# A layernorm, attention and gated projection layer on one NeuronCore: the next batch's x brought in with features on partitions, and the order of two groups' weight work

## The chip, the cores and the metric

One core of a Trainium2 chip. The metric is the device time of one launch in microseconds, the median of the runs. Engines: TensorE (PE), VectorE (DVE), ScalarE (ACT), GpSimd (POOL) and SyncE (SP, which issues nearly all DMAs).

## The reference

For x of shape (4, 512, 1024), all in float32:

```
xn = layernorm(x)                                        # over 1024 features
q, k, v = xn @ Wq.T, xn @ Wk.T, xn @ Wv.T                # 32 query heads, 8 key/value heads, head size 128
q, k = rmsnorm(q) * q_norm_w, rmsnorm(k) * k_norm_w
attn = softmax(q k' / sqrt(128) + slope[h] * (key - query), causal)
s = (attn v) @ Wo.T                                      # 4096 -> 1024
g = silu(xn @ W.T + bias + sum_n lora_weights[n] * 2 * (xn @ A_n.T) @ B_n.T)
return x + s * g
```

## The kernel before

**Precision and products.** Each float32 operand is split into a high part (a copy rounded to fp32r, by ACT) and a low part (operand minus high, by DVE or POOL), and every product is three matmuls, high-high, high-low and low-high (lines 507 to 510).

**Groups, steps.** The kernel runs 4 batches of 8 groups (one key/value head with its 4 query heads, one gate tile). A group n = 8 batch + g has 4 steps j = 0 to 3, one query head each. In this document a step is written batch.g.j, so 1.7.0 is batch 1, group 7, quarter 0. While group n is attended, the projection of group n + 1 (q, k, v, gate: 896 columns) is computed: a 2x2 block scheme of Strassen's kind with seven products P1 to P7 of sums of blocks of x (two token halves by two feature halves) with sums of blocks of the weights. A piece is one product for one tile of 128 tokens, 12 matmuls of 448 columns. Quarter 0 takes the pieces of P1 and P2, quarter 1 those of P6 and P7, quarter 2 those of P4, quarter 3 those of P5 and P3. Pieces end in one of two PSUM banks; ACT evacuates P1 and P2 (line 827), DVE adds the others into `raw` (line 1314).

**A step on PE** (lines 704 on): scores of head m mixed with probabilities times v of head m - 1; transposes of queries and keys; the pieces; output projection of head v = m - 2, columns 0 and 1; transposes of m's probabilities, rounds 0 to 2; output columns 2; round 3; output column 3. A turned tile goes through three banks in turn: ACT takes the high part (line 858), DVE the low part (line 1284) and frees the bank. Output columns are added by DVE (`add_out`, lines 1342 and 1344), which frees the bank for the next but one.

**Orders written out by hand.** Each engine runs a list; an instruction behind a waiting one waits too.
- ACT in a step: exps, head output, queries and keys high, normalising, `split_b(v + 1)` (output weights' high part, line 822; in quarter 0 behind P1's evacuation), evacuations or squares, rounds 0 to 2 of the probabilities, high parts of one product's weights (line 788), round 3, high parts of a second product's weights (not in quarter 2).
- POOL in a step: bias of the next head (line 1100; two buffers, so it waits only for the scores of the head before), `low_b(v + 1)` (line 1092), in quarters 1 and 3 of groups 1 to 5 of batch 0 the four sums of the weights of group n + 2 (lines 1132 to 1137), then two low parts for each of the weight products that ACT has split (line 1081), the ones that PE's next step begins with. In group 0 the sums come last.
- DVE in a step: scores with bias and maxima (line 1319), inverse row sums, head output, queries low, RMS factors (lines 1262 to 1267) and scalings (line 1274), pieces, `add_out` columns 0 and 1, rounds 0 to 2 low, column 2, round 3, column 3. In quarter 2 the factors of the next group stand between columns 0 and 1. In 0.0.0 it also makes the eight weight sums of group 1, and four inverses of the gate.
- SP: loads, stores and copies in the order of their use. The sums of a group's weights go to DRAM once all four are there, and the loads of later weights wait for that store.

**x of the next batch.** The first batch's x is prepared before the steps. For batches 1 to 3, one DMA brings 512 tokens on 128 partitions; DVE takes bn_stats in quarter 1 of group 5 (group 6 for batch 1), factors in the quarter after; ACT scales and shifts the four token tiles; PE transposes x in 14 rounds of 4 transposes (`turn_x`), four in quarter 3 of group 6, six in 7.0 and four in 7.1; ACT takes the high parts (14 of 512 columns) and DVE the low parts from PSUM; POOL makes the four sums of blocks in place between rounds (P7's in 6.3, those of P6, P5 and P3 in 7.0).

## Time and profile before

| what | value |
|---|---|
| median of 3 runs (lowest, highest) | 2655.3 us (2654.26, 2657.38) |
| the profiled execution, its own time | 2655.72 us |
| its span in the trace, mean granted clock | 2653.9 us, 0.995 |
| PE, DVE, ACT, POOL busy | 97%, 64%, 66%, 65% |
| chain that ended last | PE 90%, DVE 3%, DMA 2%, POOL 2%, ACT 1% |
| DMA | 414.78 MB |

The span is the time between the first and the last instruction of the profiled execution. A window's row gives, for a stretch, the busy time of PE, PE's weight loads, DVE, ACT and POOL with their instructions, then the granted clock, the DMA share and GB/s. Starts are us from the span's start. Where a stretch of a timeline waited, the idle time before it and what ended it stand in brackets. A step's start is that of its first score matmul.

### The profile page before, as it was taken

The page shows a single profiled execution, that of the slowest core. Times are in us where ns is not written, and L with a number is a line of the kernel's source. Part 1 is how long each engine was busy: PE and PEld are TensorE (multiplying, and loading weights), DVE is VectorE, ACT ScalarE, POOL GpSimd, SP SyncE. Part 2 cuts the span into 40 slices and gives each one's busy share as a digit, 9 for nine tenths or more (in the row PEclk, how much of TensorE's full clock was granted, in tenths as well). Part 3 has the DMA queues.
Part 4 walks back from the last instruction along what each step waited for, and adds up shares of the span by engine and source line. Part 5 has one row for each costly group of instructions (what it writes and reads, how often), then busy time and mean ns, then how long its engine had stood idle before and what let it go on. Part 6 is the DMA issues. An engine that isn't in the chain of part 4 may idle for free.

```text
span 2653.9 us, 39893 instructions
## 1 busy us (share of the span) xinstructions
PE 2583.1 (97%) x13840; PEld 2288.9 (86%) x13840; DVE 1699.8 (64%) x3533; ACT 1764.6 (66%) x4633; POOL 1718.0 (65%) x839
## 2 busy tenths in 40 slices
PE   6789999999999999999999999999999999999997
PEld 5778888888888888888888888888888888888886
DVE  7565656666766665666667666666666756656656
ACT  4565666767767666667766667666777666667764
POOL 3577887785767565655667756565666766656555
PEclk9899999999999999999999999999999999999999
DMA  7868878875354333433344433433334533333323
GB/s 283 289 219 278 265 261 272 271 258 166 118 171 154 113 106 118 140 112 118 106 137 155 128 119 111 144 106 118 109 104 137 189 106 108 115 116 112 112 78 131
DMA packets 171896, 414.78 MB, mean 156 GB/s; under 512 B 31024, under 2 KB 63920, under 8 KB 170800
## 3 DMA queue, kind: packets, MB, share of 16 engines
q1 hardware_dynamic: 170144, 410.19, 47.1%
q8 instruction: 112, 1.84, 0.3%
q10 hardware_dynamic: 1552, 2.04, 0.2%
q14 instruction: 88, 0.72, 0.1%
HBM read 339.81 MB, written 89.13 MB: 162 GB/s over the span
## 4 chain that ended last, share of the span: by engine, by line
PE 90%; DVE 3%; DMA 2%; POOL 2%; ACT 1%; SPq 1%; issue 0%; ACTq 0%; POOLq 0%; DVEq 0%
PE proj L508 21%; PE proj L510 21%; PE proj L509 21%; PE tr L608 5%; PE tr L588 3%; PE sc L508 3%; PE sc L509 3%; PE sc L510 3%; PE ot L509 3%; PE ot L510 3%; PE ot L508 3%; DMA wu<-xtok 1%; PE tr L581 1%; DMA wl<-wu 1%; POOL wl L1081 1%
## 5 line engine op out<-in xcount | busy, mean ns | idle before, releaser
L1081 POOL TENSOR_TENSOR wl<-wl,wh 128x896 fp32r<-128x896 f32 x428 | 909.1, 2156 | 552.3 <-ACT wh L788 552.2
L508 PE MATMUL proj<-wh,xh 128*128 128x448 f32 x1792 | 670.7, 374 | 7.3 <-ACT raw L827 2.2
L509 PE MATMUL proj<-wl,xh 128*128 128x448 f32 x1792 | 657.9, 367 | 0.0
L510 PE MATMUL proj<-wh,xl 128*128 128x448 f32 x1792 | 657.8, 367 | 0.0
L1092 POOL TENSOR_TENSOR wb_lo<-wb_lo,wb_hi 128x1024 fp32r<-128x1024 f32 x128 | 307.7, 2404 | 303.7 <-ACT wb_hi L822 303.7
L879 ACT ACTIVATE misc<-misc,negmax 128x128 f32<-128x128 f32 (+3 forms) x512 | 286.7, 565 | 266.3 <-DVE negmax L1319 266.1
L508 PE MATMUL proj<-o_hi,wb_hi 128*128 128x512 f32 x1024 | 425.2, 415 | 7.4 <-DVE acc L1344 3.5
L1344 DVE TENSOR_TENSOR acc<-acc,proj 128x512 f32<-128x512 f32 x476 | 324.8, 683 | 149.7 <-PE proj L510 147.8
L858 ACT ACTIVATE pT_hi<-tr 128x512 fp32r<-128x512 f32 (+3 forms) x512 | 197.5, 440 | 325.9 <-PE tr L608 325.9
L510 PE MATMUL proj<-o_hi,wb_lo 128*128 128x512 f32 x1024 | 403.6, 394 | 0.0
L509 PE MATMUL proj<-o_lo,wb_hi 128*128 128x512 f32 x1024 | 401.3, 392 | 0.0
L788 ACT ACTIVATE wh<-wl 128x896 fp32r<-128x896 f32 x428 | 387.9, 965 | 19.7 <-DMA wl<-wu 19.2
L1314 DVE TENSOR_TENSOR raw<-raw,proj 128x448 f32<-128x448 f32 x320 | 197.4, 617 | 301.9 <-PE proj L510 300.1
L508 PEld LDWEIGHTS proj<-wh,xh 128*128 128x128 f32 x1792 | 337.9, 189 | 37.1 <-ACT raw L827 4.9
L510 PEld LDWEIGHTS proj<-wh,xl 128*128 128x128 f32 x1792 | 337.4, 188 | 30.0
L509 PEld LDWEIGHTS proj<-wl,xh 128*128 128x128 f32 x1792 | 338.1, 189 | 27.8
L1319 DVE CUSTOM_DVE_ANT_0 misc<-sc,misc 128x128 f32<-128x128 f32 (+3 forms) x512 | 240.9, 487 | 175.9 <-PE sc L510 174.7
L1284 DVE TENSOR_TENSOR pT_lo<-tr,pT_hi 128x512 fp32r<-128x512 f32 (+3 forms) x512 | 226.6, 484 | 74.7 <-ACT pT_hi L858 74.4
L834 ACT ACTIVATE junk<-raw 128x128 f32<-128x128 f32 x640 | 189.8, 301 | 97.2 <-DVE raw L1314 93.4
L886 ACT ACTIVATE misc<-misc,rs_inv 128x128 f32<-128x128 f32 (+3 forms) x512 | 245.2, 558 | 1.0 <-DVE rs_inv L1325 1.0
L508 PEld LDWEIGHTS proj<-o_hi,wb_hi 128*128 128x128 f32 x1024 | 193.4, 189 | 51.7 <-DVE acc L1344 4.1
L1100 POOL TENSOR_SCALAR misc<-misc,slope 128x512 f32<-128x512 f32 x128 | 233.6, 1825 | 4.1 <-DMA misc<-rel 4.1
(135 smaller groups left out, 4438.1 us busy)
## 6 DMA issues: line engine op xcount, KB each, us to landing
wl<-wu SPq DMA_DIRECT2D x426, 448.0 KB, 3.9
wb_lo<-wo_in SPq DMA_DIRECT2D x128, 512.0 KB, 3.3
wu<-xtok SPq DMA_DIRECT2D x13, 1792.0 KB, 9.7
wo_in<-wo SPq DMA_DIRECT2D x32, 512.0 KB, 6.2
xtok<-wa SPq DMA_DIRECT2D x52, 256.0 KB, 4.0
wu<-xtok SPq DMA_DIRECT2D x13, 896.0 KB, 6.2
gate_dram<-misc SPq DMA_DIRECT2D x32, 256.0 KB, 5.0
xtok<-xT SPq DMA_DIRECT2D x28, 256.0 KB, 5.1
```

Source lines behind the costliest of these rows:

```text
L508: pe.matmul(out, hi_l, hi_r, start=first, stop=False, skip_group_check=onto)
L509: pe.matmul(out, hi_l, lo_r, start=False, stop=False, skip_group_check=onto)
L510: return pe.matmul(out, lo_l, hi_r, start=False, stop=last, skip_group_check=onto)
L788: act.activation(w_slot(wh, w), w_slot(wl, w, True), ACT.Copy).then_inc(w_hi_done, 1)
L879: act.activation(p, p, ACT.Exp, bias=negmax[:, i:i + 1], scale=-1.0, accum_out=rowsum[:, i:i + 1]).then_inc(exp_done, 1)
L886: ins = act.activation(p, p, ACT.Copy, scale=rs_inv[:, i:i + 1])
L1081: pool.tensor_tensor(w_slot(wl, w), w_slot(wl, w, True), w_slot(wh, w), ALU.subtract).then_inc(w_ready, 1)
L1092: pool.tensor_tensor(wb_lo[:, v % 2, :], wb_lo[:, v % 2, :].bitcast(F32), wb_hi[:, v % 2, :], ALU.subtract).then_inc(wb_ready, 1)
L1100: pool.tensor_scalar(bias_sb[:, m % 2, :], rel_sb[:], slope[:, m % H:m % H + 1], None, ALU.mult).then_inc(bias_ready, 1)
L1284: dve.tensor_tensor(dst, bank, hi, ALU.subtract).then_inc(tr_free, 1)
L1319: dve.tensor_tensor_reduce(prob[:, P_AT[i]:P_AT[i] + w], sc_ps[i % 2][:, 0:w], bias_sb[:, m % 2, S - w:S], -1.0, 3e38, ALU.add, ALU.min, n ...
L1344: dve.tensor_tensor(a, a, bank, ALU.add).then_inc(out_free, 1)
```

## The change

- x of batches 1 to 3 is loaded as `xT`, features on partitions (2 MB in one DMA, at the same places of SP's list). No transposes of it are left.
- For the statistics each token tile (512 KB) is loaded once more into a new buffer `rows`, in steps 4.3, 5.0, 5.1 and 5.2; DVE takes bn_stats there. In 5.3 the two factors per token are computed and spread over 128 columns by two copies, in 6.0 PE turns them in two rounds of four transposes, so that every partition holds the factor of each token, and DVE copies them to `rows`. In 6.1 DVE multiplies x in four parts of 1024 columns; POOL adds the shifts, parts 0 and 1 at the end of its list of 6.1, parts 2 and 3 at the end of that of 6.3, with P7's sum behind them. P6's sum stands in 7.0, P5's and P3's in 7.1, ahead of the output weights' low part.
- High and low parts of x are made a product at a time (7 of 1024 columns each on ACT and DVE), the low parts now from SBUF: P1, P2 in 6.3, P7, P4, P6 in 7.0, P5, P3 in 7.1.
- One bias buffer in place of two: the bias of the next head waits for all four scores of this one.
- Squares wait one by one for the square before last (two buffers of one head each in place of two of three heads).
- In groups 0 and 1 of batch 0, ACT takes round 3 of the probabilities right behind round 2, and the output weights' high part behind it (quarters 1 to 3). In 0.0.0 ACT's exps come ahead of three weight splits; the two sums for P4 and, in 0.0.2, group 1's first factors move behind DVE's last low part or output column; group 0's gate inverses move to quarter 1.

The diff, cut to its core, with eight columns of indentation taken off inside the builder:

```diff
 def x_fills(n, j):
+
     b, g = divmod(n, HKV)
     if b + 1 == BATCH:
 return []
-    at = {(6, 3): range(0, 4), (7, 0): range(4, 10), (7, 1): range(10, 14)}
-    return [("x", b + 1, f) for f in at.get((g, j), ())]
-
-
-def ln_group(b):
-
-    return 6 if b == 1 else 5
+    at = {(6, 3): (P1, P2), (7, 0): (P7, P4, None, P6), (7, 1): (None, P5, P3)}
+    return [(b + 1, p) if p is not None else None for p in at.get((g, j), ())]
+
+
+def x_tile(n, j):
+
+    b, g = divmod(n, HKV)
+    t = {(4, 3): 0, (5, 0): 1, (5, 1): 2, (5, 2): 3}.get((g, j))
+    return None if t is None or b + 1 == BATCH else (b + 1, t)
+
+
+def x_count(b, p):
+
+    return NP * (b - 1) + [P1, P2, P7, P4, P6, P5, P3].index(p) + 1
...
-z_buf, e_buf, rel_sb = (misc[:, PW + i * S:PW + i * S + S] for i in (2, 3, 4))
+misc = sb("misc", [P, PW + 6 * S])
+prob = misc[:, 0:PW]
+bias_sb, z_buf, e_buf, rel_sb = (misc[:, PW + i * S:PW + i * S + S] for i in range(4))
+
+rows = misc[:, PW + 4 * S:PW + 6 * S]
...
+
+def x_block(p):
+
+    chunk, at = {P1: (0, 0), P5: (0, 0), P2: (4, 0), P3: (4, 0),
+                 P7: (0, 256), P6: (0, 256), P4: (4, 256)}[p]
+    return flat(xtok).rearrange("p (k n) -> p k n", k=NK)[:, chunk:chunk + 4, at:at + 256]
+
+def x_part(i):
+
+    chunk, at = i % 2 * 4, i // 2 * 256
+    part = flat(xtok).rearrange("p (k n) -> p k n", k=NK)[:, chunk:chunk + 4, at:at + 256]
+    return part, slice(at, at + 256)
...
+        chunks = xT[b * NK:b * NK + NK].rearrange("k p n -> p k n")
+        sp.dma_start(flat(xtok).rearrange("p (k n) -> p k n", k=NK), chunks).then_inc(x_in, 16)
...
+    def load_rows(b, t):
+
+        if t > 0:
+            sp.wait_ge(row_stat, NT * (b - 1) + t)
+        elif b > 1:
+            sp.wait_ge(x_norm, 4 * (b - 1))
+        sp.dma_start(rows, x_tok[b - 1][:, t, :]).then_inc(rows_in, 16)
...
-        if g == 0 and t == 0:
+        if g == 0 and t == 0 and b == 0:
             pe.wait_ge(tr_free, LO["x", b, 2 * FILLS.index(p) + 1] + 1)
+        elif g == 0 and t == 0:
+            pe.wait_ge(x_ready, x_count(b, p))
...
+    def turn_tokens(b, i):
+
+        key = ("r", b, i)
+        pe.wait_ge(row_spread, b)
+        bank = turn_bank(key)
+        for t in range(NT):
+            at = i * S + t * P
+            mm = pe.transpose(bank[:, t * P:t * P + P], rows[:, at:at + P], ident_sb[:])
         mm.then_inc(tr_done, 1)
...
-        for u in pieces:
+        for i, u in enumerate(unit_pieces(n, j)):
             piece(*u)
-            if fills:
-                turn_x(fills.pop(0))
+            if (n % HKV, j) == (6, 0) and n + HKV < NG and i < 2:
+                turn_tokens(n // HKV + 1, i)
...
+    def x_hi_later(b, p):
+
+        if p in FILL_SUM:
+            act.wait_ge(sum_ready, 4 * b + FILL_SUM[p])
+        else:
+            act.wait_ge(x_norm, 4 * (b - 1) + {P1: 1, P2: 2, P4: 4}[p])
+        act.wait_ge(u_done, u_count(HKV * b - 1, p, 1))
+        act.activation(xh[:, p], x_block(p), ACT.Copy).then_inc(x_hi_done, 1)
...
         exps(m)
         last = n + 1 == NG
+        if m == 0:
+            split_later(P1, 1)
+            for h in range(2):
+                split_later(P2, h)
         if m > 0:
...
-        elif not last:
+        elif n >= 2 and not last:
             split_b(v + 1)
...
-                x_hi(fills.pop(0))
-            if (g, j) == (6, 3) and b == 0 and u[1] == P3:
-                ln_scale(1, 2 + u[2])
+            fill = fills.pop(0) if fills else None
+            if fill:
+                x_hi_later(*fill)
...
-            x_hi(fills.pop(0))
-        if (g, j) == (6, 1) and 0 < b < BATCH - 1:
-            for t in range(NT):
-                ln_scale(b + 1, t)
+        if (g, j) == (5, 3) and b + 1 < BATCH:
+            ln_rsqrt(b + 1)
         for k in range(3):
             probs_hi(m, k)
-        if (g, j) == (ln_group(b + 1), 1) and b + 1 < BATCH:
-            ln_rsqrt(b + 1)
-        if (g, j) == (6, 2) and b == 0:
-            ln_scale(1, 0)
-            ln_scale(1, 1)
+        if n < 2:
+            probs_hi(m, 3)
+            if j > 0:
+                split_b(v + 1)
...
+        if n >= 2:
+            probs_hi(m, 3)
         if m == 0:
...
-            wait_alone(pool, scored, 4 * m - 4)
-        pool.tensor_scalar(bias_sb[:, m % 2, :], rel_sb[:], slope[:, m % H:m % H + 1], None,
+        if m >= 1:
+            wait_alone(pool, scored, 4 * m)
+        pool.tensor_scalar(bias_sb[:], rel_sb[:], slope[:, m % H:m % H + 1], None,
                            ALU.mult).then_inc(bias_ready, 1)
...
         if what == P7:
-            pool.wait_ge(ln_ready, scaled_rows(b, 4))
             if b == 0:
+                pool.wait_ge(ln_ready, 2)
                 pool.wait_ge(x_scaled, 2)
+            else:
+                pool.wait_ge(x_norm, 4 * b)
             pool.tensor_tensor(r21, r11, r21, ALU.subtract).then_inc(sum_ready, 1)
         if what == P6:
...
+    def split_of(b, p, f):
+
+        if b == 0:
+            pool.wait_ge(tr_done, TR["x", 0, f] + 1)
+        else:
+            pool.wait_ge(x_ready, x_count(b, p))
+
+    def x_add(b, i):
+
+        part, at = x_part(i)
+        pool.wait_ge(x_mul_done, 4 * (b - 1) + i + 1)
+        pool.wait_ge(row_free, 2 * b)
+        shift = rows[:, S + at.start:S + at.stop].unsqueeze(1).to_broadcast([P, 4, 256])
+        pool.tensor_tensor(part, part, shift, ALU.add).then_inc(x_norm, 1)
...
         bias_of(m + 1)
         if j == 0 and n + 1 == NG:
             values_lo(n)
-        low_b(v + 1)
-        if (g, j) == (6, 3) and next_x is not None and b > 0:
-            x_sum(next_x, P7)
         if (g, j) == (7, 0) and next_x is not None:
             x_sum(next_x, P6)
+        if (g, j) == (7, 1) and next_x is not None:
+            x_sum(next_x, P5)
+            x_sum(next_x, P3)
+        low_b(v + 1)
         if j == 0 and n + 1 < NG:
             values_lo(n)
-        if (g, j) == (7, 0) and next_x is not None:
-            x_sum(next_x, P5)
-            x_sum(next_x, P3)
         if j in (1, 3) and n > 0 and n + 2 < HKV:
             weight_sums(n + 2, j // 2)
...
             low_product(*[(n + 1, P6), (n + 1, P4), (n + 1, P3), (n + 2, P1)][j])
-        if (g, j) == (6, 3) and b == 0:
-            x_sum(1, P7)
         if m > 0 and j != 2:
             low_product(*[(n + 1, P7), (n + 1, P5), None, (n + 2, P2)][j])
+        if (g, j) == (6, 1) and next_x is not None:
+            x_add(next_x, 0)
+            x_add(next_x, 1)
+        if (g, j) == (6, 3) and next_x is not None:
+            x_add(next_x, 2)
+            x_add(next_x, 3)
+            x_sum(next_x, P7)
         if j == 3 and n + 1 == NG:
             for c in range(4, NK):
...
+    def row_stats(b, t):
+
+        dve.wait_ge(rows_in, 16 * (NT * (b - 1) + t + 1))
+        for i in range(2):
+            ins = dve.bn_stats(bn[:, t, 6 * i:6 * i + 6], rows[:, 512 * i:512 * i + 512])
+        ins.then_inc(row_stat, 1)
+        if t == NT - 1:
...
+    def spread_rows(b):
+
+        dve.wait_ge(ln_newton, 5 * (b + 1))
+        for i, column in enumerate((rinv_x, shift_x)):
+            place = rows[:, i * S:i * S + S].rearrange("p (t n) -> p t n", t=NT)
+            ins = dve.tensor_copy(place, column[:].unsqueeze(2).to_broadcast([P, NT, P]))
+        ins.then_inc(row_spread, 1)
+
+    def take_rows(b, i):
+        dve.wait_ge(tr_done, TR["r", b, i] + 1)
+        dve.tensor_copy(rows[:, i * S:i * S + S], tr_ps[TR["r", b, i] % 3][:]).then_inc(row_free, 1)
+
+    def x_mul(b, i):
+
+        part, at = x_part(i)
+        dve.wait_ge(x_in, 16 * b)
+        dve.wait_ge(row_free, 2 * b - 1)
+        factor = rows[:, at].unsqueeze(1).to_broadcast([P, 4, 256])
+        dve.tensor_tensor(part, part, factor, ALU.mult).then_inc(x_mul_done, 1)
+
+    def x_lo_later(b, p):
+        dve.wait_ge(x_hi_done, x_count(b, p))
+        dve.tensor_tensor(xl[:, p], x_block(p), xh[:, p], ALU.subtract).then_inc(x_ready, 1)
...
         if j == 0 and more:
             queries_lo(n, 1)
             if n == 0:
-                weight_sum(1, 0, P7)
-                weight_sum(1, 0, P6)
+                for h in range(2):
+                    for p in (P5, P7, P6):
+                        weight_sum(1, h, p)
...
-                weight_sum(1, 0, P4)
-                weight_sums(1, 1)
         if not more:
...
-        late_gate = g == 7 and next_x
+        late_gate = g == 7 and next_x or n == 0
...
             if turned:
-                x_lo(turned.pop(0))
-            if fills:
-                turned.append(fills.pop(0))
+                x_lo_later(*turned.pop(0))
+            fill = fills.pop(0) if fills else None
+            if fill:
+                turned.append(fill)
+            if (g, j) == (6, 0) and next_x and i < 2:
+                take_rows(b + 1, i)
             if (j, p, t) == (0, P2, 0):
...
+        if x_tile(n, j):
+            row_stats(*x_tile(n, j))
         if turned:
-            x_lo(turned.pop(0))
+            x_lo_later(*turned.pop(0))
         add_out(v, 0)
-        if turned:
-            x_lo(turned.pop(0))
-        if j == 2 and more:
+        if j == 2 and n > 0:
             row_factors(n + 1, 0)
-        if j == 2 and g == ln_group(b + 1) and next_x:
+        if (g, j) == (5, 3) and next_x:
             ln_factors(b + 1)
+            spread_rows(b + 1)
         add_out(v, 1)
...
         add_out(v, 2)
         probs_lo(m, 3)
         add_out(v, 3)
+        if m == 0:
+            for h in range(2):
+                weight_sum(1, h, P4)
+        if m == 2:
+            row_factors(1, 0)
```

## Rows read from the trace of the kernel before

**Rows 1.** The page, part 1: busy time, share of the span, instructions.
```profile
PE 2583.1 (97%) x13840; PEld 2288.9 (86%) x13840; DVE 1699.8 (64%) x3533; ACT 1764.6 (66%) x4633; POOL 1718.0 (65%) x839
```

**Rows 2.** Windows of steps 1.6.1 and 1.6.2: window, length, busy time (instructions), clock, DMA share.
```profile
1244.60:1265.78 21.18, 21.18 (x115) 18.91 (x114) 11.15 (x25) 15.91 (x29) 12.33 (x7) 1.00 0.35 112
1265.78:1281.06 15.28, 15.28 (x83) 13.56 (x82) 9.14 (x25) 12.68 (x36) 12.73 (x7) 1.00 0.30 95
```

**Rows 3.** Windows, 0.6.2 to 0.7.1, 1.5.2 to 1.7.1, 2.5.2 to 2.7.1.
```profile
625.04:713.33 88.29, 86.07 (x481) 75.59 (x480) 61.56 (x124) 65.53 (x163) 57.34 (x28) 1.00 0.38 124
1186.32:1351.56 165.24, 164.38 (x906) 145.93 (x904) 105.10 (x229) 118.97 (x305) 104.89 (x51) 1.00 0.34 107
1824.56:1989.70 165.14, 164.28 (x905) 145.95 (x904) 105.07 (x228) 118.97 (x305) 104.88 (x51) 1.00 0.34 107
```

**Rows 4.** Windows of steps 1.5.2, 1.6.3, 1.7.0 and 1.7.1.
```profile
1186.32:1202.24 15.92, 15.70 (x83) 13.41 (x82) 9.83 (x30) 13.11 (x38) 13.18 (x7) 1.00 0.30 92
1281.06:1304.04 22.98, 22.98 (x131) 20.48 (x130) 16.52 (x32) 14.85 (x45) 11.46 (x6) 1.00 0.37 116
1304.04:1328.69 24.65, 24.00 (x139) 21.22 (x138) 14.59 (x32) 19.70 (x49) 20.74 (x11) 1.00 0.31 97
1328.69:1351.56 22.87, 22.87 (x132) 20.51 (x130) 16.64 (x33) 13.38 (x29) 12.21 (x7) 1.00 0.34 104
```

**Rows 5.** Windows of steps 0.0.0, 0.1.1, 0.1.2 and 0.1.3.
```profile
84.66:113.91 29.25, 17.77 (x79) 15.16 (x78) 22.82 (x32) 17.45 (x51) 18.98 (x9) 0.84 0.78 272
202.01:227.65 25.64, 22.83 (x116) 20.24 (x115) 11.14 (x25) 13.83 (x28) 19.05 (x10) 0.93 0.87 291
227.65:245.20 17.55, 16.15 (x84) 13.42 (x82) 11.02 (x25) 12.88 (x36) 16.26 (x9) 1.00 0.86 297
245.20:266.41 21.21, 21.21 (x116) 18.93 (x115) 12.91 (x27) 13.22 (x41) 15.98 (x9) 1.00 0.72 236
```

**Rows 6.** Timeline of ACT, late in step 0.1.3: start, length, instruction.
```profile
253.84 1.06 ACT L822 ACTIVATE wb_hi<-wb_lo 128x1024 fp32r<-128x1024 f32 x1
...
266.00 0.29 ACT L858 ACTIVATE pT_hi<-tr 128x128 fp32r<-128x128 f32 x1
```

**Rows 7.** Timeline of POOL, 0.1.1 to 0.1.3.
```profile
229.56 8.37 POOL L1081 TENSOR_TENSOR wl<-wl,wh 128x896 fp32r<-128x896 f32 x4
...
254.97 2.40 POOL L1092 TENSOR_TENSOR wb_lo<-wb_lo,wb_hi 128x1024 fp32r<-128x1024 f32 x1 [5.15 <-ACT wb_hi L822]
257.32 2.12 POOL L1132 TENSOR_TENSOR xtok<-xtok 128x896 f32<-128x896 f32 x1
...
265.79 8.38 POOL L1081 TENSOR_TENSOR wl<-wl,wh 128x896 fp32r<-128x896 f32 x4
```

**Rows 8.** Timeline of PE, start of step 0.2.0.
```profile
270.97 0.45 PE L508 MATMUL proj<-wh,xh 128*128 128x448 f32 x1
...
271.46 0.37 PE L510 MATMUL proj<-wh,xl 128*128 128x448 f32 x1
271.67 0.37 PE L508 MATMUL proj<-wh,xh 128*128 128x448 f32 x1
```

**Rows 9.** Timeline of PE, end of step 0.0.0; in brackets the idle time before.
```profile
113.79 0.48 PE L608 MATMUL tr<-ident_sb,misc 128*128 128x128 f32 x1 [6.02 <-DVE pT_lo L1284]
```

**Rows 10.** Timeline of ACT, end of step 0.0.1.
```profile
137.91 2.06 ACT L788 ACTIVATE wh<-wl 128x896 fp32r<-128x896 f32 x2 [3.28 <-DMA wl<-wu]
```

**Rows 11.** Timeline of DVE, step 0.0.2.
```profile
149.67 1.94 DVE L1267 SCALAR_TENSOR_TENSOR tmp<-tmp,rinv 128x12 f32<-128x12 f32 x1
```

**Rows 12.** Timeline of POOL, step 1.7.0.
```profile
1302.98 8.39 POOL L1081 TENSOR_TENSOR wl<-wl,wh 128x896 fp32r<-128x896 f32 x4 [6.56 <-ACT wh L788]
```

**Rows 13.** Timeline of ACT, step 1.7.0.
```profile
1312.66 0.54 ACT L827 ACTIVATE raw<-proj 128x448 f32<-128x448 f32 x1
...
1314.24 0.55 ACT L827 ACTIVATE raw<-proj 128x448 f32<-128x448 f32 x1 [0.55 <-PE proj L510]
```

**Rows 14.** DVE's line 1274: count, ns minimum/median/maximum, first and last start.
```profile
L1274 DVE SCALAR_TENSOR_TENSOR raw<-raw,tmp x160: 676/684/2619, 75.4 to 2585.4; 128x512 f32<-128x512 f32 x160
```

120 lines of the change are left out of this document (55 added, 65 removed).

## The prediction

> **What bounds the kernel now.** I read the page first: TensorE (PE) is busy for 97% of the span, and every other engine stands near 65% [rows 1]. So only two things move the end: PE work that goes, and stretches in which PE stands. Steps are named batch.group.quarter. A step of quarter 1 takes 21.18 us and one of quarter 2 takes 15.28 with PE busy throughout [rows 2]; quarters 0 and 3 are as long as quarter 1 where nothing is added. Whatever is above that is the price of something extra. Three stretches, one per batch up to the end of its quarter 7.1, show the price of preparing the next x: batch 0 needs 88.29 us from 0.6.2 on against 15.28 + 3 x 21.18 = 78.82, batches 1 and 2 need 165.24 and 165.14 against 2 x 15.28 + 6 x 21.18 = 157.64 [rows 3]. That is 9.47 + 7.60 + 7.50 = **24.6 us**, nearly all for 168 transposes and their bank changes (1.6.3, 1.7.0 and 1.7.1 take 1.80, 3.47 and 1.69 too long, 1.5.2 takes 0.64) [rows 4]. It is all that this half of the change can win. The other half works in groups 0.0 and 0.1, where steps are far from full: 0.0.0 has PE busy for 17.77 of 29.25 us [rows 5].
>
> **Part one, output weights behind turned probabilities (groups 0.0 and 0.1).** ACT's split of the output weights moves from the middle of a step to behind the last turned probabilities. POOL's order does not change: bias, low half of the output weights, then in 0.1.1 and 0.1.3 the four weight sums, and only then the low halves that PE's next step starts with. In 0.1.3 the split begins at 253.84 today [rows 6], POOL subtracts at 254.97, sums from 257.32 to 265.8, and goes straight on with the four weight slots [rows 7], just ahead of PE, which starts its product at 270.97 [rows 8]. The sums fit only because the split is early. Afterwards the split follows the last probabilities, which ACT ends at 266.00 + 0.29 = 266.3 [rows 6]. Then: split 1.06 to 267.3, low half 2.40 to 269.7, four sums 8.5 to 278.2, first slot 2.1 to 280.3, second 2.1 to 282.4 (8.38 for four). PE can begin at 280.3 and needs the second slot half a piece later (6 of the piece's 12 matmuls, at 0.207 each from 271.46 and 271.67: 1.24 us [rows 8]): it should have had that at 272.2. **Stall 10.2 us.** In 0.1.1 the same happens: now the first of the four slots starts at 229.56 [rows 7], 1.9 us into 0.1.2 (start 227.65) [rows 5]; moved, with the last probabilities split at 227.5 (as shortly ahead of the next step as in 0.1.3), it is 227.5 + 1.06 + 2.4 + 8.5 = 239.4, the second ends at 243.6 against a need at 232.9: 10.7 us, less the 0.9 that is lost there already, so **9.8**. Bounds of the two together: 18 (the sums' DMA wait moves nothing) to 21. In group 0.0 the sums come last in POOL's list and the later split costs PE only some 1.3 us, at the start of 0.1.0.
>
> **Part two, P4's sums.** In 0.0.0 PE waits 6.02 us for a bank that DVE frees only after the weight sums and the gate inverses [rows 9]. Two sums move behind, the inverses go to quarter 1, ACT's exps come ahead of three splits: 5.0 us saved by following each engine to 0.0.1. But the store of the sums starts about 7 us later, and the transfers behind it hold ACT at 137.91 (idle 3.28 for a load) before the exps of 0.0.2 [rows 10]; with PE earlier, that landing is late next and takes the 5 back and by my reading 1.2 more. In 0.0.2 DVE's tiny factor instructions stand behind POOL's sums (this one takes 1.94 us for 12 columns) and hold up PE by 5.1 [rows 11]; behind the last output they hold up the next scores by some 2.0 instead. With 1.3 for 0.1.0 I take -5.0 + 6.2 - 5.1 + 2.0 + 1.3 = **-0.6**, bounds -7 (the landing comes as early as PE does) and +4 (it comes late by the store's whole 7): this is the softest term. The early groups together: -0.6 + 9.8 + 10.2 = **+19.4**.
>
> **Part three, x with features on partitions.** The 24.6 go. In their place, for each of three batches:
> - x.6.0: two rounds of four token transposes, 0.45 each as today's rounds (1.80 for four) [rows 4]: 0.9. Bounds 0.9 and 1.1.
> - x.5.2 and x.5.3: bn_stats, variance, Newton steps and the two copies now stand ahead of an output addition that frees PE's bank, and the last two ahead of the turned probabilities' low halves. From the position of PE's need each comes 0.9 late: 1.8. Bounds 0.6 and 2.8.
> - x.6.1: four multiplications on DVE of 128x1024 between pieces; 1.2 each, an estimate from the 0.68 of 512 elements [rows 14], which with the evacuation fit into the 12 x 0.207 = 2.48 of a piece: 0.2. Bounds 0 and 1.
> - x.6.2: POOL's additions 0 and 1 come behind low halves that end 7.3 us into the next step, so run to 12.1; DVE's factor instructions, as in rows 11, wait behind them: 1.2. Bounds 0 and 1.5.
> - x.6.3: DVE's low half of P1 waits for ACT and then for POOL's output weights, and the piece behind it is evacuated late: 0.7. Bounds 0 and 1.5.
> - x.7.1: two x low halves and two inverses around pieces: 1.1. Bounds 0 and 3.
> - **x.7.0**, where it is decided. POOL's list of x.6.3 now ends with additions 2 and 3 and the sum for P7, behind the low halves of the next weights. Those start only when ACT has split them, and in 1.7.0 they end at 1302.98 + 8.39 = 1311.37 [rows 12], 7.33 us into the step. Three operations of 2.40 (what POOL takes for 1024 elements [rows 7]) bring P7's sum to 14.5 at the least. ACT, in order, evacuates P1's first token tile 8.6 into the step [rows 13], then must split P7 of the next x, and waits. The second tile of P1 (today 10.2 into the step [rows 13]) stays in PSUM until 14.5 + 1.0 + 0.5 = 16.0 (a split of 1024 [rows 6] and the evacuation), while PE needs it for P2 at 4.56 [rows 5, 8] + 3 x 2.48 = 12.0: **4.0 us**. Behind it ACT has P4's split, an exp, the output weights, v and P6's split, which waits for the next sum: output columns 0 and 2 come another 1.8 late. Sum 5.8 at the least. With DVE and POOL blocking each other (below) P7's sum ends at 15.8 and the step is 8.7 over. I take 7.5.
>
> Per batch 0.9 + 1.8 + 0.2 + 1.2 + 0.7 + 1.1 + 7.5 = 13.4, so 40.2 for three; less 24.6 is **+15.6**. Bounds: 3 x 7.3 - 24.6 = -2.7 and 3 x 19.6 - 24.6 = +34. Squares with a wait each, the single bias buffer and the 6 MB of row loads I cost at nothing: the bias now waits for the step's last score, and POOL comes to it only at 7.3 today [rows 12]; the square before last has long ended when the next one starts; DMA is at 0.34 in the later batches [rows 3]. If DMA cover goes (batch 0), a late load costs PE its lateness, 1 to 3 us.
>
> On blocking: a DVE scaling of 512 elements from SBUF takes 0.68 us in the median and up to 2.62, always where POOL is in an operation [rows 14]. x's low half is now read from SBUF twice (x and its high half), no longer from PSUM. The Trainium skill, page "SBUF — State Buffer", section "Who interferes with whom", says that a DVE instruction with two SBUF inputs and a GpSimd instruction that reads SBUF exclude each other for a whole instruction, one with a single SBUF input does not. By that rule each new low half would meet a full block, x.7.0 would cost 8.7 and the time would be 2694.3.
>
> **The sum.** 2655.7 (the profiled execution, 0.4 above the median of 2655.3) + 19.4 + 15.6 = **2690.7**, or 2691. Its own range, with the ends not all at once: 2669 to 2707.
>
> **The rivals.**
> - *Both waits are covered* (ends faster). Place: PE's queue in 0.2.0 and x.7.0. If POOL is free so early that the first product of 0.2.0 starts within 1 us of its place and P7's sum is there at 9.2 in x.7.0, the transposes decide: 2655.7 - 5 - 24.6 + 3 x 2.9 = 2634.8. For it: POOL is idle a third of the span. Against: its list is written out, and rows 7 and 12 leave no gap. Chance 0.14.
> - *Only x is covered*: 2655.7 + 19.4 - 24.6 + 3 x (2.7 to 5.9) = 2659 to 2668. Against: ACT's order. Chance 0.10.
> - *Only the early groups are covered*: 2655.7 - 0.6 + 15.6 = 2670.7. Chance 0.08.
> - *DMA becomes the bound in batch 0*, where rows for x and later stores meet a queue that is 0.86 to 0.87 busy [rows 5]: some 3 us in four steps, 2700 and above. Chance 0.05.
> - The forecast: 0.63.
>
> **How the numbers follow.** Bounds of two tenths of a per cent are 2650 and 2660.6 (about what this kernel's measurement can tell from no change). Faster 0.14 from the first rival; same 0.04, the low end of the second; slower 0.82. The range leaves out the first rival and little else: 2658 to 2707.
>
> **What would show it.** Right: 0.1.2 near 26 us and 0.2.0 near 31, PE idle in both for a POOL low half; x.7.0 near 29 with PE waiting for ACT's evacuation of P1, and ACT waiting for POOL's sum; x.7.1 without transposes under 22.9. PE's instructions fall by 144. Wrong: 0.2.0 at 21.2; x.7.0 under 24.65; or POOL starting P7's sum before 9 us into x.7.0.

## The result and the profile after

The changed kernel takes **2708.6 us** (median of 4 runs, 2707.05 to 2713.97) against 2655.2 for the kernel before (4 runs, 2654.26 to 2657.38): ratio 1.0204, 95% interval 1.0186 to 1.0221. That is 53.4 us more; the forecast was 2691 with a range of 2658 to 2707. The sign was right, the size 18 us short, the median 1.6 us outside the range. The profiled execution took 2713.97 us, 5.4 above its median, at a mean granted clock of 0.984 against 0.995 before; so the steps below, read from it, add up to more than the 53.4. Of the runs below, one execution each of `x_only` and `sum_early` took 11471 and 7367 us; these two are in no ratio, and without them the medians are 2687.4 and 2696.5.

The page of the changed kernel, part 1, which answers to [rows 1]:

```profile
PE 2590.5 (96%) x13696; PEld 2287.9 (84%) x13696; DVE 1778.9 (66%) x3536; ACT 1752.7 (65%) x4600; POOL 1729.3 (64%) x851
```

PE has 144 instructions fewer, as forecast, and is busy 7 us longer: it ran more often at the lower of its two clock levels. DVE has 79 us more of busy time in about as many instructions. At the shortest length that each kind of them shows, they would need only 6 us more than before; the rest, over 60 us, is time that an instruction spends waiting once it is under way.

The windows of steps 0.1.0 to 0.1.2, 0.2.0, 0.5.3, 0.6.0, 1.6.0, 1.7.0 to 1.7.2 and 2.7.2 of the changed kernel (window, length, busy time of each engine with its instructions, granted clock, DMA share, GB/s), to be read beside [rows 2, 4, 5]:

```profile
178.01:207.74 29.73, 24.09 (x115) 20.59 (x114) 22.66 (x29) 17.32 (x44) 25.80 (x13) 0.89 0.46 164
207.74:229.48 21.74, 21.38 (x115) 18.86 (x114) 10.87 (x24) 10.74 (x24) 9.21 (x5) 1.00 0.95 318
229.48:256.80 27.32, 18.26 (x83) 15.99 (x82) 9.02 (x25) 12.81 (x38) 20.36 (x10) 0.81 0.50 172
279.27:310.65 31.38, 23.18 (x116) 20.30 (x114) 19.93 (x29) 18.05 (x46) 26.01 (x13) 0.84 0.56 181
586.26:618.04 31.78, 22.94 (x116) 19.71 (x115) 23.87 (x35) 15.50 (x46) 20.97 (x11) 0.88 0.57 188
618.04:641.26 23.22, 23.22 (x123) 20.77 (x122) 14.47 (x31) 15.02 (x41) 9.33 (x6) 0.94 0.72 240
1263.29:1285.33 22.04, 22.04 (x124) 19.70 (x122) 14.59 (x31) 15.96 (x43) 13.08 (x8) 1.00 0.35 108
1345.47:1374.79 29.32, 24.47 (x116) 21.16 (x115) 25.23 (x29) 19.86 (x47) 25.88 (x12) 0.88 0.27 81
1374.79:1397.95 23.16, 21.66 (x116) 18.87 (x115) 18.33 (x29) 13.01 (x26) 16.38 (x9) 1.00 0.32 103
1397.95:1415.21 17.26, 15.70 (x84) 13.50 (x82) 10.75 (x26) 12.63 (x36) 12.56 (x7) 1.00 0.27 85
2043.91:2062.73 18.82, 17.23 (x84) 14.88 (x82) 10.78 (x26) 12.64 (x36) 12.59 (x7) 0.91 0.25 78
```

Two things stand out. 0.5.3 (fifth row), where the forecast allowed under 2 us, takes 31.78 us instead of 21.21. And 0.6.0 (sixth row) has PE busy for all of its 23.22 us, at a granted clock of 0.94: the clock fell to its lower level during the stall in 0.5.3, at 610.4, and rose again at 620.6, 2.6 us into 0.6.0. The same step of batch 1 (seventh row), with the same eight token transposes, takes 22.04 us at full speed; so 1.2 us are the clock's and 0.9 the transposes', which the forecast has.

This is where the time goes in 0.5.3: DVE first, then POOL in the same stretch, then PE (timeline: start, length, instruction):

```profile
602.72 0.69 DVE L1451 TENSOR_TENSOR acc<-acc,proj 128x512 f32<-128x512 f32 x1 [0.76 <-PE proj L545]
603.72 1.34 DVE L1296 TENSOR_TENSOR tmp_x<-rinv_x 128x4 f32<-128x4 f32 x1 [0.32 <-ACT rinv_x L971]
605.10 2.04 DVE L1298 TENSOR_TENSOR tmp_x<-tmp_x,var_x 128x4 f32<-128x4 f32 x1
607.18 0.17 DVE L1300 TENSOR_SCALAR tmp_x<-tmp_x 128x4 f32<-128x4 f32 x1
607.38 1.91 DVE L1302 TENSOR_TENSOR rinv_x<-rinv_x,tmp_x 128x4 f32<-128x4 f32 x1
609.33 1.99 DVE L1304 SCALAR_TENSOR_TENSOR shift_x<-mv,rinv_x 128x4 f32<-128x4 f32 x1
611.36 2.26 DVE L1340 COPY misc<-rinv_x 128x512 f32<-128x512 f32 x1
613.54 0.41 DVE L1340 COPY misc<-shift_x 128x512 f32<-128x512 f32 x1
613.87 0.67 DVE L1451 TENSOR_TENSOR acc<-acc,proj 128x512 f32<-128x512 f32 x1
614.47 1.47 DVE L1391 TENSOR_TENSOR pT_lo<-tr,pT_hi 128x512 fp32r<-128x512 f32 x3
```

```profile
600.85 2.13 POOL L1202 TENSOR_TENSOR xtok<-xtok 128x896 f32<-128x896 f32 x1 [1.26 <-DMA wu<-xtok]
602.94 2.11 POOL L1203 TENSOR_TENSOR xtok<-xtok 128x896 f32<-128x896 f32 x1
605.00 2.13 POOL L1205 TENSOR_TENSOR xtok<-xtok 128x896 f32<-128x896 f32 x1
607.21 2.07 POOL L1207 TENSOR_TENSOR xtok<-xtok 128x896 f32<-128x896 f32 x1
609.24 4.09 POOL L1131 TENSOR_TENSOR wl<-wl,wh 128x896 fp32r<-128x896 f32 x2
```

```profile
615.20 0.47 PE L656 MATMUL tr<-ident_sb,misc 128*128 128x128 f32 x1 [8.77 <-DVE pT_lo L1391]
```

Each of the four long four-column instructions starts while one of POOL's operations is in progress and ends when that one ends. They then alternate: by the time DVE's next instruction starts, POOL has begun its next. The short one, at 607.18, started in the gap between two POOL operations, 0.03 us ahead of the second. Behind the chain stand the copies, the second output addition (613.87) and only then the low halves of the turned probabilities (614.47). The first of these frees the bank that PE needs for round 3: PE waits 8.8 us.

1.7.0 went as forecast. POOL and ACT there:

```profile
1346.48 6.30 POOL L1131 TENSOR_TENSOR wl<-wl,wh 128x896 fp32r<-128x896 f32 x3
1352.73 4.75 POOL L1196 TENSOR_TENSOR xtok<-xtok,misc 128x1024 f32<-128x1024 f32 x2
1357.56 2.87 POOL L1170 TENSOR_TENSOR xtok<-xtok 128x1024 f32<-128x1024 f32 x1
```

```profile
1354.08 0.54 ACT L872 ACTIVATE raw<-proj 128x448 f32<-128x448 f32 x1
1360.46 1.06 ACT L916 ACTIVATE xh<-xtok 128x1024 fp32r<-128x1024 f32 x1 [5.84 <-POOL xtok L1170]
1361.42 0.53 ACT L872 ACTIVATE raw<-proj 128x448 f32<-128x448 f32 x1
```

P7's sum ends 15.0 us into the step (forecast 14.5 at the least, 15.8 with blocking), ACT has waited 5.84 for it, and P1's second tile is evacuated at 16.0 to 16.5, where the forecast had it at 16.0. Of the signs that the prediction named, 0.1.2, 0.2.0 and x.7.0 came; only 1.7.1 missed, with 23.16 us in place of under 22.9.

### The profile page after: what moved, and what is told of

It is laid out like the page before. It is cut to its first block, busy times and chain, and to the rows that moved or that the text cites. A ratio compares the mean times of both kernels' runs of the same rounds, so it can differ in the third digit from the quotient of the medians.

```text
span 2712.2 us, 39613 instructions
## 1 busy us (share of the span) xinstructions
PE 2590.5 (96%) x13696; PEld 2287.9 (84%) x13696; DVE 1778.9 (66%) x3536; ACT 1752.7 (65%) x4600; POOL 1729.3 (64%) x851
## 3 DMA queue, kind: packets, MB, share of 16 engines
q10 hardware_dynamic: 1552, 2.04, 0.2%
## 4 chain that ended last, share of the span: by engine, by line
PE 82%; DVE 6%; POOL 5%; ACT 2%; DMA 2%; issue 1%; SPq 1%; ACTq 0%; POOLq 0%; DVEq 0%
PE proj L543 20%; PE proj L545 20%; PE proj L544 19%; PE tr L656 4%; PE tr L626 3%; PE sc L543 3%; PE sc L545 3%; PE sc L544 3%; PE ot L544 3%; PE ot L545 3%; PE ot L543 2%; POOL wl L1131 1%; DMA wl<-wu 1%; DVE xl L1357 1%; DVE raw L1381 1%
## 5 line engine op out<-in xcount | busy, mean ns | idle before, releaser
L833 ACT ACTIVATE wh<-wl 128x896 fp32r<-128x896 f32 x428 | 387.7, 965 | 16.6 <-DMA wl<-wu 16.3
L1150 POOL TENSOR_SCALAR misc<-misc,slope 128x512 f32<-128x512 f32 x128 | 204.5, 1597 | 99.1 <-DVE negmax L1426 95.4
## 6 DMA issues: line engine op xcount, KB each, us to landing
wu<-xtok SPq DMA_DIRECT2D x13, 1792.0 KB, 10.2
```

The lines of the kernel that those rows point to most:

```text
L833: act.activation(w_slot(wh, w), w_slot(wl, w, True), ACT.Copy).then_inc(w_hi_done, 1)
L1150: pool.tensor_scalar(bias_sb[:], rel_sb[:], slope[:, m % H:m % H + 1], None, ALU.mult).then_inc(bias_ready, 1)
```

## The experiments

Each run shared its chip with runs of the kernel before, whose medians were 2654.6 to 2655.6. Steps are again batch.group.quarter.

**The two halves.** In `x_only` all edits to the early groups are undone; in `start_only` they are the only ones; `g0_only` has them, but with ACT's split behind the turned probabilities in group 0.0 alone:

```
-                elif n >= 2 and not last:
+                elif n >= 1 and not last:
```

> The changed kernel with everything of the early groups put back as before (ACT's splits of the output weights in the middle of a step in groups 0.0 and 0.1, the order of DVE's weight sums, gate inverses and row factors in group 0.0); only the new preparation of x stays. Theory (the two halves add up): the trace of the changed kernel has 23.1 us of its extra time in 0.0.0 to 0.2.0 and 34.9 in the three stretches that prepare x, so this kernel stands some 23 us below the changed one, 2686 us, with 0.5.3 near 32 us and x.7.0 near 29. Rival (the halves feed each other: the early lateness pushes POOL and the DMA queues late in all of batch 0): 0.5.3 and 0.7.0 shrink too and the time is under 2678. Second rival (the x half costs little by itself, the stalls of TensorE's clock come from the early groups): 2665 or less.

> The kernel before with the early groups changed alone; x is prepared as before, with 168 transposes. Theory (the halves add up): 2655.2 + 23 = 2678 us, with 0.1.2 near 27 us, 0.2.0 near 31, and batches 1 to 3 as before. By the forecast of the prediction it would be 2655 + 19.4 = 2674.6. Rival (the lateness of 0.1.0, 29.73 us against 24.53 before, belongs to the x half through its buffers or the single bias buffer): 0.1.0 stays near 24.5 and the time is 2672 or less.

> The changed kernel with the output weights behind the turned probabilities in group 0.0 only; in group 0.1 they stand in the middle of the step again. Theory (POOL's four weight sums stand behind the late low half of the output weights and ahead of the low halves that PE's next step needs): 0.1.2 falls from 27.3 to some 17.5 us, 0.2.0 from 31.4 to 21.2, and the time is 20 us less, 2689. Rival (the sums wait for their DMA anyway, as 0.1.0 already ran 5 us late): 0.1.2 stays above 23 and the time falls by less than 12.

Measured: `x_only` 2687.6 (ratio 1.0122, 1.0102 to 1.0142), `start_only` 2680.0 (1.0096, 1.0080 to 1.0111), `g0_only` 2690.7 (1.0133, 1.0118 to 1.0148). Against the kernel before that is 32.0 and 24.5, sum 56.5 for 53.4: the halves add up within 3 us. Of the early half 17.9 (2708.6 - 2690.7) is the split in group 0.1: 0.1.2 is back from 27.32 to 18.98, 0.2.0 from 31.38 to 21.18. 0.1.0 is long (28.84) in `start_only` too, so it belongs to the early half.

**P4's sums alone.** `start_dve` is the kernel before with part two of the change and ACT's output-weight splits where they were.

> The kernel before with only part two of the change: P4's weight sums behind the last output addition of 0.0.0, ACT's exps ahead of three splits, the gate inverses of group 0.0 in quarter 1, the row factors of group 0.1 at the end of 0.0.2; ACT's splits of the output weights stay where they were. The prediction gave this part about -1.9 us (its -0.6 without the 1.3 for the later split). Theory (0.0.0 gains 6 us and 0.0.1 to 0.1.0 give it back, 0.1.0 above all, where DVE's row factors and scalings now meet POOL's weight sums): 2655 to 2660. Rival (the late split of the output weights in group 0.0 caused the loss of 0.1.0): 0.1.0 back at 24.5 us, the time 2649 to 2653.

Measured 2660.1 (1.0022, 1.0013 to 1.0032): slower by 5. 0.0.0 gains 6.2 (23.08 from 29.25), 0.0.1 gives it back (26.28 from 18.84), and 0.1.0 is 25.81 against 24.53. The other 3 us of 0.1.0 in `start_only` come with ACT's late split; the forecast had 1.3 for them. In the changed kernel PE waits 5.1 us there for an output addition, behind a scaling pair of 5.10 us (3.23 before) and a tensor_scalar of 2.30 (0.41 before), both beside POOL's sums. Its edit, in DVE's list (ACT's three first splits and the gate inverses move with it):

```
                 add_out(v, 3)
+                if m == 0:
+                    for h in range(2):
+                        weight_sum(1, h, P4)
+                if m == 2:
+                    row_factors(1, 0)
```

**What stalls 0.1.2 and 0.2.0.** `g1_sums_behind` moves POOL's weight sums of group 0.1 behind the low halves; `g1_narrow_sums` leaves them in place and cuts their time:

```
-                if j in (1, 3) and n > 0 and n + 2 < HKV:
+                if j in (1, 3) and n > 1 and n + 2 < HKV:
...
+                if j in (1, 3) and n == 1:
+                    weight_sums(3, j // 2)
```

```
+                if g == 3:
+                    b11, b12, b21, b22 = (t[:, :, 0:4] for t in (b11, b12, b21, b22))
```

> The changed kernel with POOL's weight sums of group 0.1 (for group 3) behind the low halves of the next weights. ACT's late split of the output weights stays. Theory (the prediction's sum: 1.06 for the split, 2.4 for the low half, 8.5 for the sums, 2.1 for the first slot): with the 8.5 us of sums out of the way the first slot is ready about when PE needs it, the second some 1.7 us after; 0.1.2 falls from 27.3 to 17.5 to 20, 0.2.0 from 31.4 to 21.2 to 23.5, the time by 15 to 20 us to 2689 to 2694. Rival (the late split alone is enough to stall PE): 0.2.0 stays above 27 and the time falls by less than 8.

> The changed kernel with POOL's eight weight sums for group 3, which it does in 0.1.1 and 0.1.3, cut to 8 columns each; all else, the order and every wait, stays. The weights of group 3 are not the reference's. Theory (8.5 us of sums between the late split of the output weights and the low halves that PE needs next are the stall of 0.1.2 and 0.2.0; moving them behind only handed the lateness on, to the next bias and low halves): 0.1.2 from 27.3 to 17.5 to 19.5, 0.2.0 from 31.4 to 21.2 to 23.5, 0.1.3 no longer than 22.5; the time 14 to 19 us less, 2690 to 2695. Rival (in POOL's list the split alone is late enough): 0.2.0 above 27, less than 8 us gained.

The first missed: 2712.8 (1.0219, 1.0202 to 1.0236), nothing gained. 0.1.2 fell to 20.21, but 0.1.3 rose to 29.89 and 0.2.0 stayed at 29.48. POOL after that move (timeline; 0.1.3 starts at 251.75):

```profile
246.49 2.09 POOL L1205 TENSOR_TENSOR xtok<-xtok 128x896 f32<-128x896 f32 x1
248.66 2.11 POOL L1207 TENSOR_TENSOR xtok<-xtok 128x896 f32<-128x896 f32 x1
250.75 1.57 POOL L1150 TENSOR_SCALAR misc<-misc,slope 128x512 f32<-128x512 f32 x1
252.28 2.41 POOL L1142 TENSOR_TENSOR wb_lo<-wb_lo,wb_hi 128x1024 fp32r<-128x1024 f32 x1
```

The bias, which the scores of 0.1.3 wait for, now stands behind the sums, and in 0.1.3 ACT waits 8.3 us for a load of weights at a DMA share of 0.90. The second came as expected: 2691.4 (1.0141, 1.0126 to 1.0156), 0.1.2 at 17.84, 0.2.0 at 22.70, 0.1.3 unchanged at 22.47. 0.1.1 rose from 21.74 to 24.74. So it is the sums' 8.5 us behind a late split. In either order POOL has 2.4 + 8.5 + 8.4 and a bias of 1.6 behind the split, 20.9 us of a step of 21.2; that no other order would do is argued from this sum, not measured.

**P7's sum in x.7.0.** `sum_early` moves three POOL operations ahead of the low halves of x.6.3:

```
+                if (g, j) == (6, 3) and next_x is not None:
+                    x_add(next_x, 2)
+                    x_add(next_x, 3)
+                    x_sum(next_x, P7)
                 if m == 0:
...
```

> The changed kernel with POOL's additions 2 and 3 and its sum for P7 ahead of the low halves of the next weights in x.6.3, and nothing else moved. In 1.6.3 POOL stands idle for 7.6 us between the output weights and those low halves, and the three operations take 7.2. Theory (ACT's wait for P7's sum in x.7.0 holds P1's second evacuation and through it PE): x.7.0 falls from 28.2 / 29.3 / 29.3 us to 22 to 24.7, the time by 13 to 21 us, to 2688 to 2695. Rival (the low halves of the weights, pushed back, are late next: PE needs them 4.6 us into x.7.0): x.7.0 stays above 27 and the time falls by less than 6. Second rival (the clock, not the wait, makes x.7.0 long): PE's matmuls there stay at half clock and x.7.0 stays above 26.

Measured 2697.2 (1.0156, 1.0139 to 1.0173), 11.4 less, where 13 to 21 was expected. x.7.0 fell to 22.27, 23.39 and 22.30: the forecast's mechanism is shown. x.6.3 rose from 22.6 to 24.5, where DVE's low half of P2 now meets POOL's additions (DVE, then POOL):

```profile
1332.10 2.88 DVE L1357 TENSOR_TENSOR xl<-xtok,xh 128x1024 fp32r<-128x1024 f32 x1
1334.90 0.61 DVE L1421 TENSOR_TENSOR raw<-raw,proj 128x448 f32<-128x448 f32 x1
```

```profile
1330.52 6.69 POOL L1196 TENSOR_TENSOR xtok<-xtok,misc 128x1024 f32<-128x1024 f32 x2
```

**0.5.3.** `newton_early` puts DVE's Newton steps and spread copies at the start of x.5.3; `sums_late` leaves DVE's code alone and moves POOL's four sums of 0.5.3 behind the low halves (as in `g1_sums_behind`, with `m == 23` as the step).

```
                     keys_lo(n + 1)
                     queries_lo(n + 1, 0)
+                if (g, j) == (5, 3) and next_x:
+                    ln_factors(b + 1)
+                    spread_rows(b + 1)
```

> The changed kernel with the Newton steps for x and the two spread copies (and ACT's logarithm and exponential ahead of them) at the beginning of x.5.3, where POOL stands idle, in place of behind the first output addition. Theory (each of DVE's four-column instructions with two SBUF inputs waits for one of POOL's weight sums of 2.1 us, and the next output addition stands behind all of them): 0.5.3 falls from 31.8 us to 21.2 to 22.2, 0.6.0 by up to 1 (the clock no longer falls at its end), 5.3 in batches 1 and 2 by at most 0.5; the time by 10 to 12 us, to 2697 to 2699. Rival (0.5.3 is long because POOL's low halves of the weights or the sums' DMA are late): 0.5.3 stays above 28 and the time falls by less than 3. Second rival (the instructions cost as much wherever they stand, now ahead of the pieces' evacuations): under 5 us gained.

> The changed kernel with one thing moved: in 0.5.3 POOL's four weight sums for group 7 stand behind the low halves of the next weights, not ahead of them. DVE's code is untouched, its Newton steps for x stand where the change put them. Theory (they are long only because a POOL operation is in progress when each is due): without the sums POOL is idle from the output weights to some 617.5 us, the four-column instructions take 0.16 us each and 0.5.3 falls from 31.8 us to 21.2 to 23.5; time less by 8 to 11 us, 2698 to 2701. Rival (the instructions are slow in that place for a reason of their own, or the lateness comes from the output weights): 0.5.3 stays above 28, time within 3 us of the changed kernel. Late next, possibly: the sums reach DRAM 8 us later and 0.6.0 or 0.6.1 gets longer.

`newton_early`: 2703.6 (1.0186, 1.0169 to 1.0203), 5 us less in place of 10 to 12. 0.5.3 fell to 23.28, but 5.3 of batches 1 and 2 rose from 21.7 to 23.3: ahead of the pieces' evacuations the instructions cost 1.6. `sums_late`: 0.5.3 at 21.72. The same DVE instructions (timeline):

```profile
601.45 0.16 DVE L1298 TENSOR_TENSOR tmp_x<-rinv_x 128x4 f32<-128x4 f32 x1 [0.30 <-ACT rinv_x L971]
601.65 0.16 DVE L1300 TENSOR_TENSOR tmp_x<-tmp_x,var_x 128x4 f32<-128x4 f32 x1
602.44 0.43 DVE L1342 COPY misc<-rinv_x 128x512 f32<-128x512 f32 x1
```

1.34, 2.04 and 2.26 us have become 0.16, 0.16 and 0.43 by a change on POOL alone: the cause is shown. The time moved only to 2705.3 (1.0189, 1.0174 to 1.0204), 3 us less in place of 8 to 11, as 0.6.0 and 0.6.1 grew to 25.05 and 23.53 us. In 0.6.0 the moved sums meet the RMS factors of eight columns (1.80, 2.03 and 2.05 us); in 0.6.1 ACT waits up to 4.0 us for a load of weights.

Which instruction of the chain pays depends on which engine starts first. In `x_only` the second product started in the gap and took 0.16 us, and the tensor_scalar of four columns with one input, 0.17 in the changed kernel, started 0.17 us behind POOL's next sum (DVE, then POOL):

```profile
582.25 1.96 DVE L1294 TENSOR_SCALAR tmp_x<-tmp_x 128x4 f32<-128x4 f32 x1
```

```profile
582.08 2.11 POOL L1201 TENSOR_TENSOR xtok<-xtok 128x896 f32<-128x896 f32 x1
```

**Can the x half pay?** `x_fixed` is `x_only` with both moves. `x_fixed2` spreads POOL's operations over x.6.1 to x.6.3. `x_tuned` also multiplies in 6.0 and takes P1's and P2's halves in x.6.2, with the Newton steps early in batch 0 alone; `x_tuned_g` puts the gate product of x.7.1 behind the last output addition. POOL's list in `x_fixed2`, ahead of the low halves, and `x_tuned`'s other places:

```
+                if g == 6 and j > 0 and next_x is not None:
+                    if j < 3:
+                        x_add(next_x, 2 * j - 2)
+                        x_add(next_x, 2 * j - 1)
+                    else:
+                        x_sum(next_x, P7)
```

```
-    at = {(6, 3): (P1, P2), (7, 0): (P7, P4, None, P6), (7, 1): (None, P5, P3)}
+    at = {(6, 2): (P1, P2), (7, 0): (P7, P4, None, P6), (7, 1): (None, P5, P3)}
...
-                    if (g, j) == (6, 1) and next_x:
-                        x_mul(b + 1, i)
+                    if (g, j) == (6, 0) and next_x and i > 1:
+                        x_mul(b + 1, i - 2)
+                    if (g, j) == (6, 1) and next_x and i < 2:
+                        x_mul(b + 1, i + 2)
```

> The new preparation of x alone (early groups as before), with both moves: additions 2, 3 and the sum for P7 early in x.6.3, Newton steps and spread copies at the beginning of x.5.3. Theory (the stalls add up): 2687.6 less the 11.4 that the first move gave, less some 10 of the second: 2666 us, with x.7.0 near 22.3 and 0.5.3 near 21.5; so still 10 us slower than before, because x.6.3 (24.5), x.7.1 (22.9) and x.7.2 (17.1) keep their excess, which rests on DVE and POOL waiting for each other. Rival (transposes were the dear part, the rest is noise): 2650 us or less.

> As x_fixed, with POOL's six operations for x spread over its three idle stretches: additions 0 and 1 ahead of the low halves of x.6.1, 2 and 3 ahead of those of x.6.2, the sum for P7 ahead of those of x.6.3. Theory (x.6.3 is long because DVE's low half of P2 meets POOL's additions, 2.88 us in place of 1.21, and a piece's evacuation stands behind it; x.6.2 because row factors meet additions 0 and 1): x.6.3 falls from 24.5 to some 22.5, x.6.2 from 16.3 to 15.5, the time by 6 to 9 us against x_fixed, to 2657 to 2660, even with the kernel before or just above it. Rival (x.6.3 is long because x's high and low halves themselves crowd ACT and DVE): x.6.3 stays at 22.8 or above and the gain is under 5 us.

> The new preparation of x alone (early groups as before) with its work spread anew: the multiplications in 6.0 and 6.1, additions 0 and 1 ahead of the low halves of x.6.1, the high and low halves of P1 and P2 in x.6.2 in place of x.6.3, additions 2, 3 and P7's sum ahead of the low halves of x.6.3, Newton steps early in batch 0 alone. Theory (x.6.3 is long by 3.1 us because DVE's low half of P2 meets an addition of POOL; x.5.3 of batches 1 and 2 was better where the change had it): x.6.3 at some 22.7, x.5.3 of batches 1 and 2 at 21.7, x.6.2 up to 1 us longer; 2671.3 - 3 - 4 + 2 = 2666 us. Rival (each move only trades one meeting of DVE and POOL for another): 2669 or more.

> As x_tuned, with DVE's gate product of x.7.1 behind the last output addition. In 2.7.1 of the changed kernel it takes 2.61 us in place of 0.68 beside a low half of POOL's, and the last output additions, probabilities and scores stand behind it. Theory: x.7.2 falls from 16.3 to 18.8 us to 15.3 to 15.8, 3 to 6 us in three batches. Rival (POOL's next low half blocks it as long behind the additions, and the next scores stand behind it): x.7.2 at 17 or more, no gain.

`x_fixed` 2671.3 (1.0059, 1.0044 to 1.0074), 5 above what was expected, mostly the 1.6 us in 5.3 of each later batch and x.7.0 at 25.0 and 24.8 in batches 1 and 2. The next two missed: 2691.8 (1.0142, 1.0127 to 1.0157) and 2692.7 (1.0144, 1.0129 to 1.0159). In `x_fixed2` x.6.2 takes 23.0 us (and x.6.1 23.4), for row factors of twelve columns meet the additions (DVE in 1.6.2):

```profile
1297.60 2.31 DVE L1362 TENSOR_TENSOR tmp<-rinv 128x12 f32<-128x12 f32 x1 [0.23 <-ACT rinv L897]
1299.94 2.28 DVE L1364 SCALAR_TENSOR_TENSOR tmp<-ss,tmp 128x12 f32<-128x12 f32 x1
1302.26 1.99 DVE L1367 SCALAR_TENSOR_TENSOR tmp<-tmp,rinv 128x12 f32<-128x12 f32 x1
```

In `x_tuned` 0.6.0 takes 38.19 us: DVE's first multiplication waits 15.2 us for the load of x, and the output additions stand behind it. The change itself multiplies in 6.1, where x is there in time and the step takes 21.18 us. x.6.2 also takes 19.9 to 21.1 us, in place of up to 1 more than 16.3. `x_tuned_g` is 2683.2 (1.0106, 1.0091 to 1.0122), 9.5 less than `x_tuned`. x.7.2 fell from 17.1 to 15.8, so the gate product's place counts, but only for 3.9 us in three batches; the rest of the gain is in other steps (0.6.2, 1.6.3, 1.7.0 among them) and was not traced to a cause.

`x_narrow` cuts POOL's additions and sums for x of batches 1 to 3 to 8 elements, so it leaves most of that work out; `x_best` joins the better places; its row factors of x.6.2 move too.

```
-                    r11, r12, r21, r22 = (x_block(p) for p in (P1, P2, P7, P4))
+                    r11, r12, r21, r22 = (x_block(p)[:, :, 0:2] for p in (P1, P2, P7, P4))
```

```
-                if j == 2 and more:
+                if j == 2 and more and g != 6:
                     row_factors(n + 1, 0)
...
                 add_out(v, 3)
+                if j == 2 and more and g == 6:
+                    row_factors(n + 1, 0)
```

> The new preparation of x alone (as x_only, 2687.6 us), with POOL's additions and sums for x cut to a few columns (8 elements in a partition in place of 1024); x of batches 1 to 3 is not the reference's. It bounds what any other place for POOL's eight operations in each batch could give. Theory (the x half is dear through POOL's part: ACT's wait for P7's sum, and DVE instructions that wait for POOL): x.7.0 falls to 22.5 or less, x.6.2, x.6.3 and x.7.2 to within 1 us of 15.28, 21.18 and 15.28; 0.5.3 stays at 30 to 32, it has another cause; the time is 2655 to 2668. Rival (ACT and DVE themselves are too full there, POOL or not): x.7.0 above 24.5 and the time above 2675.

> The new preparation of x alone with what each run so far showed to be the better place: in batches 1 and 2 two multiplications in x.6.0 and two in x.6.1, additions 0 and 1 ahead of the low halves of x.6.1, P1's halves in x.6.2 and P2's in x.6.3; in batch 0 these as the change has them; additions 2, 3 and P7's sum ahead of the low halves of x.6.3, the row factors of x.6.2 and the gate product of x.7.1 behind the last output addition, the Newton steps early in batch 0 alone. Theory: excess over full steps of some 12 us in batch 0 and 8 to 9 in batches 1 and 2, together 28 to 30 against 24.6 before: 2658 to 2662 us. Rival (each move hands its wait on): 2668 or more. Below 2653 it would beat both kernels.

`x_narrow`: **2647.7** (0.9976, 0.9965 to 0.9987), 40 us below `x_only` and 7 below the kernel before, with 0.5.3 still at 29.92. Its windows of 1.6.3, 1.7.0, 1.7.1 and 1.7.2:

```profile
1283.20:1304.86 21.66, 21.60 (x115) 18.77 (x114) 16.92 (x30) 14.93 (x43) 8.12 (x5) 1.00 0.41 122
1304.86:1326.25 21.39, 21.39 (x116) 18.94 (x114) 13.70 (x29) 19.08 (x46) 16.52 (x12) 1.00 0.37 111
1326.25:1347.46 21.21, 21.21 (x116) 18.93 (x115) 16.30 (x31) 13.06 (x27) 12.49 (x9) 1.00 0.37 112
1347.46:1362.75 15.29, 15.29 (x84) 13.57 (x82) 9.15 (x25) 12.67 (x36) 12.74 (x7) 1.00 0.30 96
```

ACT and DVE still have all their own work, and each of these steps is full within 0.5 us: the loss lies in POOL's eight operations in each batch. `x_best` came to 2669.4 (1.0058, 1.0041 to 1.0075), by the rival: in 0.6.3 the row factors, moved behind the last output addition, met two of POOL's low halves (2.00 and 1.99 us) and held up the scores, 28.90 us.

So `x_dve_add` takes the additions from POOL to DVE, with P7's sum early, the Newton steps early in batch 0 alone and the gate product behind the last output addition:

```
+                    if (g, j) == (6, 2) and next_x:
+                        x_add(b + 1, i)
+                    if (g, j) == (6, 3) and next_x and i in (0, 3):
+                        x_add(b + 1, 2 if i == 0 else 3)
```

> The new preparation of x alone with its four additions of the shift on DVE (an estimate of 1.2 us each, from the multiplications of the same shape, against POOL's 2.4): 0 and 1 behind the pieces of x.6.2, 2 and 3 behind the first and the last piece of x.6.3; POOL keeps the four sums, P7's ahead of the low halves of x.6.3; the Newton steps early in batch 0, the gate product of x.7.1 behind the last output addition. Theory (the x half is dear through POOL's part, 40 us by the run with POOL's operations cut short, and four of its eight operations go): x.6.2 under 16, x.6.3 22 to 23.5, x.7.0 22.3, x.7.2 15.8; excess of about 7 us in batches 1 and 2 and 9 in batch 0, 23 us against 24.6 before: 2651 to 2657 us. Rival (DVE's additions meet POOL's other operations and come late themselves): 2662 or more.

Measured **2652.3** (median of 11 runs, 2650.09 to 2653.89) against 2655.5: ratio 0.9988, interval 0.9979 to 0.9997. It does the whole computation, with the early groups as in the kernel before, and is faster than both kernels, by about 3 us than the kernel before. How much of the 19 us between it and `x_fixed` (2671.3) is the additions' new place was not measured by itself, since the gate product and two batches' Newton steps moved too. Its windows from 1.6.2 to 1.7.2:

```profile
1264.51:1280.76 16.25, 15.50 (x84) 13.48 (x82) 13.14 (x27) 12.79 (x36) 14.91 (x7) 1.00 0.28 90
1280.76:1301.94 21.18, 21.18 (x116) 18.91 (x114) 18.23 (x31) 15.00 (x43) 9.79 (x6) 1.00 0.38 125
1301.94:1324.21 22.27, 21.47 (x115) 18.94 (x114) 17.17 (x29) 19.80 (x47) 19.24 (x10) 1.00 0.35 107
1324.21:1347.10 22.89, 21.44 (x115) 18.87 (x114) 18.00 (x30) 12.99 (x26) 16.09 (x8) 1.00 0.32 104
1347.10:1362.86 15.76, 15.55 (x83) 13.49 (x82) 9.25 (x25) 12.64 (x36) 12.65 (x7) 1.00 0.29 93
```

## Why the prediction was right in sign and short in size

By steps of the profiled executions, 57.5 us in place of 35.0:

- *Early groups*: forecast +19.4, measured +23.1. 0.1.2 came to +9.8 (forecast 9.8) and 0.2.0 to +10.2 (forecast 10.2). The wait is the one named, but both matches are partly luck. In 0.2.0 PE waits 8.2 us for POOL's low half, not 10.2, and the other 2.0 are matmuls at half clock (busy 23.18 where a step has 21.2). In 0.1.2 PE stands for 9.1 us in place of 1.4 before, which is 7.7, and its matmuls take 2.1 more (busy 18.26 against 16.15). 0.0.0 to 0.1.1 was forecast at -0.6 and came to +1.9, 0.1.3 at nothing and came to +1.3. The soft term's sign was wrong, as `start_dve` shows by itself: part two loses 5 us, and the late split takes 3 in 0.1.0 where 1.3 was forecast.
- *x.7.0*: forecast 22.5 in three batches, measured 7.0 + 8.1 + 8.2 = 23.3, by the mechanism named; `sum_early` removes 5.9 to 7.0 of each. Here too the size is partly luck: in 1.7.0 PE waits 4.3 us for P1's evacuation (forecast 4.0) and 0.6 for an output addition (forecast 1.8), and 3.3 of the step is slower matmuls (24.47 busy), which the sum did not have.
- **The step that failed is x.5.2 and x.5.3**: forecast 1.8 per batch with bounds of 0.6 and 2.8, together 5.4; measured 13.7, of which 10.6 stand in 0.5.3. The term reckons with no POOL operation. It leaves out POOL's weight sums of batch 0, which run in that quarter: each instruction that starts during a sum lasts until the sum ends. `sums_late` shows it, with 0.5.3 at 21.72. The row on which part two rested [rows 11] shows what such an instruction costs beside the sums, and the forecast applied it to 0.0.2 and x.6.2 alone. In batches 1 and 2, where there are no sums, x.5.3 is over by 0.5.
- **A second step that failed is x.7.2**: put at nothing, without a reason; measured 1.0 + 2.0 + 3.5 = 6.5. DVE's gate product takes 2.61 us in 2.7.1, in place of 0.68, ahead of the last output additions. Its removal to a place behind them gives 1.3 a batch in `x_tuned_g`.
- *The rest of x*: x.6.0 to x.6.3 11.2 against 9.0, x.7.1 4.3 against 3.3. x.6.1 costs nothing, x.6.2 1.0, as bounded; 1.2 of the excess of 0.6.0 is the clock.
- *The clock* was not in the sum. Its deficit grew from 0.005 x 2653.9 = 13 us to 0.016 x 2712.2 = 43 us of full-speed time. Not all of this is lost, since PE also stands in such stretches, but 0.6.0 alone lost 1.2 us to it with PE never waiting.

On the block between DVE and POOL: x's low half from SBUF took 1.21 us alone and up to 3.46 beside POOL; in the kernel before, from PSUM and of half the size, none took over 0.69. The Trainium skill, page "SBUF — State Buffer", section "Who interferes with whom", has it that a DVE instruction with two SBUF inputs contends with a GpSimd instruction that reads SBUF, and the trace agrees. The same section adds what the prediction left out, that a copy or a tensor_scalar in a two-port mode contends as well; the spread copy's 2.26 us, 0.43 without POOL, agrees with it. By a full block for each low half the prediction would have had x.7.0 at 8.7; the measured 7.0 to 8.2 lie below it, clock included, and P7's sum ended at 15.0 in place of 15.8.

The rivals: "only x is covered" fell with x.7.0, "only the early groups are covered" with 0.1.2 and 0.2.0, and "both are covered" with either. DMA did not become the bound: in the steps of batch 0 PE's waits end with POOL, DVE or ACT, and ACT's own waits for those weights are 16.3 us in all, 19.2 before. But a load of weights is late next in `sums_late` (ACT waits up to 4.0 us) and `g1_sums_behind` (8.3).

What stays open: x.7.1 keeps 1.7 us of excess in `x_dve_add`, where PE waits 1.5 us for a piece's evacuation. In `x_narrow` the step takes 21.2, so it hangs on POOL's operations; which of them was not taken apart. Nor was it measured how much of the 30 us of clock deficit goes with the stalls.

## What to carry to other kernels

Price an instruction on DVE by what POOL does at that moment, not by its size: here four tiny instructions in a chain cost four POOL operations, and they hold up whatever frees the bottleneck engine's bank. Before making an item late in the list of an in-order engine that is busy 65% of the time, add up what stands behind it inside one step; here it was 20.9 of 21.2 us, and the one other order that was run gained nothing. An experiment that only shortens an operation in place tells more than one that moves it, since each move here made something else late.

## What was not expected of the hardware

- A chain of four-column DVE instructions alternates with POOL's operations, and each that starts while one is in progress lasts until it ends: 1.34, 2.04, 1.91 and 1.99 us, against 0.16 each with POOL idle. One that starts in the gap between two of them is free: the tensor_scalar between them took 0.17 us, and 1.96 in `x_only`, where POOL was first.
- Additions and subtractions of two inputs, one of them in PSUM, showed none of it: the output addition never took more than 0.69 us, beside POOL or not.
- POOL pays too: two of its additions took 6.69 us beside DVE's low halves and 4.75 elsewhere.
- A stall can cost twice: after PE waited 8.8 us in 0.5.3, the next step, with PE busy throughout, took 23.22 us at a granted clock of 0.94, in place of 22.04 for the same work at 1.00 in 1.6.0. In `x_only` the clock had risen again by the end of 0.5.3, and 0.6.0 took 22.11.
